# Gated cross-attention: keys split ahead of the diagonal, one product of the denominators a batch, taken in the next batch's step

## The reference

```python
qn = layernorm(x, ln_q_g, ln_q_b)
q = qn @ Wq * scale                       # 16 heads of 64
k, v = jnp.split(media @ Wkv, 2, axis=-1) # media: the context, 1500 keys
sim = jnp.einsum('bhid,bhjd->bhij', q, k)
sim = jnp.where(media_mask[:, None, None, :], sim, neg_inf)
attn = jax.nn.softmax(sim, axis=-1)
out = jnp.einsum('bhij,bhjd->bhid', attn, v)
x = x + jnp.tanh(attn_gate) * (out @ Wo)
h = jax.nn.gelu(layernorm(x, ln_ff_g, ln_ff_b) @ W1, approximate=False) @ W2
x = x + jnp.tanh(ff_gate) * h
```

## Time and profile before

| | |
|---|---|
| median of three executions | 1866.57 us |
| profiled execution | 1864.18 us, its span 1862.4 us |
| mean granted TensorE clock | 0.939 |
| busy: PE, DVE, ACT, POOL | 1596.7, 1010.7, 613.7, 515.2 us |
| 15 steps from batch 0 to the start of batch 15, first pass | 242.8 us, PE busy 225.3, DVE 126.4 |
| the same, second pass | 242.1 us |

### The profile page before, as it was taken

One profiled execution on the slowest core, in us unless ns is written; L12 is line 12 of the kernel. 1 busy time (PEld: TensorE's weight loads), 2 busy tenths in 40 slices (PEclk: granted clock), 3 DMA queues, 4 the chain that ended last, 5 costly groups with the idle time before them and its releaser, 6 DMA issues.

```text
span 1862.4 us, 29181 instructions
## 1 busy us (share of the span) xinstructions
PE 1596.7 (86%) x8106; PEld 829.9 (45%) x8107; DVE 1010.7 (54%) x1645; ACT 613.7 (33%) x992; POOL 515.2 (28%) x365
## 2 busy tenths in 40 slices
PE   7666588988988969989977898899986988999988
PEld 3233254554554534446633444444343444444434
DVE  6786467777777735213446555455323654555440
ACT  1131155555555530025532333333030322333211
POOL 1524056766766740000001022222001022222000
PEclk9877589999999979989988899999998989999999
DMA  6000512222222112013110000000031000000000
GB/s 220 0 1 1 125 50 70 65 79 64 67 78 62 30 42 77 0 59 108 66 60 19 1 28 26 25 25 2 1 93 55 1 18 18 25 25 18 2 1 20
DMA packets 46769, 80.37 MB, mean 43 GB/s; under 512 B 8616, under 2 KB 38584, under 8 KB 46648
## 3 DMA queue, kind: packets, MB, share of 16 engines
q1 hardware_dynamic: 46648, 78.96, 14.3%
HBM read 56.82 MB, written 0.92 MB: 31 GB/s over the span
## 4 chain that ended last, share of the span: by engine, by line
PE 72%; DVE 14%; issue 8%; ACT 2%; SPq 2%; POOL 1%; DVEq 1%; DMA 1%; ACTq 0%; POOLq 0%
PE psum L1705 21%; PE psum L2159 8%; PE psum L1859 5%; PE psum L2134 3%; PE psum L2165 3%; PE psum L1894 3%; DVE WA L1381 3%; PE psum L2259 3%; PE psum L2136 2%; PE psum L2020 2%; PE psum L1833 2%; PE psum L2151 2%; PE psum L1879 2%; SPq L530 2%; PE psum L2154 2%
## 5 line engine op out<-in xcount | busy, mean ns | idle before, releaser
L1381 DVE TENSOR_REDUCE WA<-psum 112x1 f32<-112x500 f32 x384 | 243.8, 676 | 75.9 <-PE psum L1859 73.4
L773 POOL TENSOR_TENSOR XN<-XN,WBZ 125x896 f32<-125x896 f32 x128 | 266.3, 2080 | 41.2 <-ACT WBZ L981 38.2
L981 ACT ACTIVATE WBZ<-psum 125x896 f32<-125x896 f32 x192 | 174.5, 917 | 173.3 <-PE psum L1879 166.4
L1119 ACT ACTIVATE WA<-psum,y_bias 125x448 f32<-125x448 f32 x192 | 120.7, 633 | 285.5 <-PE psum L2154 285.4
L2159 PE MATMUL psum<-WA,ctxN 125*128 125x448 f32 x384 | 181.0, 552 | 8.1 <-ACT WA L1119 8.1
L1859 PE MATMUL psum<-R 128*112 128x500 f16 x384 | 157.7, 414 | 32.7 <-DVE WA L1381 21.9
L804 POOL TENSOR_TENSOR XN<-const,y_max 112x896 bf16<-112x896 f32 x32 | 53.7, 1679 | 476.0 <-PE psum L2159 348.2
L1596 DVE TENSOR_REDUCE y_max<-psum 112x1 bf16<-112x375 f32 x256 | 130.9, 532 | 100.2 <-PE psum L2136 78.8
L2134 PE MATMUL psum<-XB,R 128*112 128x375 f16 x256 | 89.5, 350 | 32.9 <-DVE y_max L1596 24.5
L1879 PE MATMUL psum<-R 128*125 (+1 forms) x768 | 109.3, 266 | 0.7 <-ACT R L948 0.7
L1604 DVE RECIPROCAL WBZ<-WBZ (+1 forms) x68 | 104.4, 1540 | 2.3 <-DVE WBZ L1625 2.3
(11 more groups left out here) (256 smaller groups left out, 2744.3 us busy)
## 6 DMA issues: line engine op xcount, KB each, us to landing
R<-WA SPq DMA_DIRECT2D x192, 62.5 KB, 2.0
ctxT<-in_ctxT SPq DMA_DIRECT2D x12, 750.0 KB, 4.2
R<-in_ctxT SPq DMA_DIRECT2D x12, 750.0 KB, 5.5
WA<-in_ctxT SPq DMA_DIRECT2D x8, 750.0 KB, 4.1
R<-WA SPq DMA_DIRECT2D x192, 31.2 KB, 1.8
ctxT<-in_ctxT SPq DMA_DIRECT2D x32, 187.5 KB
ctxN<-in_ctx SPq DMA_DIRECT2D x32, 187.5 KB
WBZ<-in_x_w SPq DMA_DIRECT2D x4, 1024.0 KB, 6.5
```

Source lines behind the costliest of these rows:

```text
L773: nc.gpsimd.tensor_tensor(z_sum[p][0:TK, :], first[0:TK, :], z_p[t % 4][0:TK, :], ALU.add)\
L981: nc.scalar.activation(z_p[t % 4][0:TK, :].rearrange("p (k n) -> p k n", k=2), psum[0:TK, s:s + 2, 0:2 * GC], ACT.Exp, scale=float(CHD0) * ...
L1119: nc.scalar.activation(y_pT[t][0:TK, g * HALF:(g + 1) * HALF], bank[2 + u % 3][0:TK, 0:HALF], ACT.Exp, bias=y_bias[0:TK, bass.ds(b * NT + ...
L1381: V.tensor_reduce(z_mx[0:PR, r, c:c + 1], bank[4 + k % 2][0:PR, 0:PC], AX_X, ALU.max)\
```

## The change

POOL splits the keys of batch b + 2 ahead of the diagonal of b + 1, as soon as the first product of values of batch b - 1 is done. PE's second `sums` goes. DVE adds tile 2 to `y_sum` as well (`add_last`, at the end of its step, once the last exponential is there), and PE takes the one product left, `denominators(b)`, in the next step, between values 0 and behind 2. It reads the `y_sum` of batch b - 1. DVE's copy of bank 7 moves with it, from the end of the step to the place between maximum 1 and invert 0. ACT's first exponential of a step waits for the two adds of the batch before instead of its product. The first step of a pass now has such a product and copy too, and one more stands behind the last step. The code for further chunks is changed to match.

```diff
@@ gpsimd, step
+                    if nxt2:
+                        wait_alone(pool, "x2_pv", PARTS * (l * B + b) + 1)
+                        keys(b + 2, (s + 2) % SLOTS)
                     wait_alone(pool, "x2_pv", PARTS * (l * B + b) + PARTS)
                     if nxt:
                         diagonal(b + 1, 1 - p)
-                    if nxt2:
-                        keys(b + 2, (s + 2) % SLOTS)
...
@@ scalar, step
                             wait_alone(act, "x2_pv", PARTS * (l * B + b) + PARTS)
-                            wait_alone(act, "x2_dn", l * B + b + 1)
+                            wait_alone(act, "x2_dsum", 2 * (l * B + b) + 2)
...
@@ vector
-                def invert(b, g):
-
-                    if g == 0:
-                        wait_alone(dve, "x2_den", l * B + b + 1)
-                    part = y_den[:, bass.ds(b, 1), g * HALF // 2:(g + 1) * HALF // 2].rearrange("p b n -> p (b n)")
+                def denominators(k):
+
+                    wait_alone(dve, "x2_dn", l * (B + 1) + k + 1)
+                    V.tensor_copy(y_den[:, bass.ds(k, 1), :].rearrange("p b n -> p (b n)"), bank[7][:, 0:HALF])\
+                        .then_inc(sem("x2_den"), 1)
+                    wait_alone(dve, "x2_den", l * (B + 1) + k + 2)
+
+                def invert(k, g):
+                    part = y_den[:, bass.ds(k, 1), g * HALF // 2:(g + 1) * HALF // 2].rearrange("p b n -> p (b n)")
                     V.reciprocal(part, part).then_inc(sem("x2_inverted"), 1)
...
+                def add_last(b):
+                    wait_alone(dve, "x2_expd", PARTS * (l * B + b) + PARTS + 3)
+                    wait_alone(dve, "x2_dsum", 2 * (l * B + b) + 3)
+                    V.tensor_tensor(y_sum[0:TK, :], y_sum[0:TK, :], y_pT[2][0:TK, :], ALU.add)\
                         .then_inc(sem("x2_dsum"), 1)
...
                         if j == 1:
+                            denominators(b)
                             invert(b, 0)
...
-                    wait_alone(dve, "x2_dn", l * B + b + 2)
-                    den = y_den[:, bass.ds(b + 1, 1), :].rearrange("p b n -> p (b n)")
-                    V.tensor_copy(den, bank[7][:, 0:HALF]).then_inc(sem("x2_den"), 1)
+                    add_last(b)
...
                 over_batches(dve, batch)
+                denominators(B)
...
@@ tensor
-                def sums(src, rows, start, stop, dst):
-
+                def denominators(k):
+
+                    wait_alone(pe, "x2_dsum", 2 * (l * B + k) + 2)
+                    wait_alone(pe, "x2_den", l * (B + 1) + k + 1)
                     for j in range(2):
-                        mm = pe.matmul(dst[HDX * j:HDX * (j + 1), 0:HALF], ones[0:rows, 0:HDX],
-                                       src[0:rows, :].rearrange("p (r j s) -> p j r s", r=PAIRS, j=2)[:, j],
-                                       start=start, stop=stop)
-                    return mm
+                        mm = pe.matmul(bank[7][HDX * j:HDX * (j + 1), 0:HALF], ones[0:TK, 0:HDX],
+                                       y_sum[0:TK, :].rearrange("p (r j s) -> p j r s", r=PAIRS, j=2)[:, j],
+                                       start=True, stop=True)
+                    mm.then_inc(sem("x2_dn"), 1)
...
                     values(0)
+                    denominators(b)
                     behind(2)
...
                     values(4)
-                    wait_alone(pe, "x2_dsum", l * B + b + 1)
-                    wait_alone(pe, "x2_den", l * B + b + 1)
-                    sums(y_sum, TK, True, False, bank[7])
                     values(5)
-                    sums(y_pT[2], TK, False, True, bank[7]).then_inc(sem("x2_dn"), 1)
...
                 over_batches(pe, step)
+                denominators(B)
```

More of the change, by code:

```diff
@@ L492, in build @@
         PARTS = 2 * KT
-        EXTRA = 47
+        EXTRA = 49
         def over_batches(eng, step):
@@ L1167, in _ @@
             dve.sem_inc(sem("x2_den"), 1)
+            dve.sem_inc(sem("x2_dsum"), 2)
             V = nc.vector
@@ L1550, in _ @@
             more = entry(dve, T_MORE, MORE)
-            V.memset(y_den[:, 0, :], 1.0).then_inc(sem("x2_first_den"), 1)
-            dve.wait_ge(sem("x2_first_den"), 1)
+            V.memset(y_sum, 1.0).then_inc(sem("x2_first_sum"), 1)
             BX = 8
@@ L1641, in extra @@
                         for g in range(2):
-                            V.tensor_copy(y_wide[:, g * HALF:(g + 1) * HALF], bank[2 + g][:, 0:HALF])
-                        V.tensor_tensor(den, den, bank[4][:, 0:HALF], ALU.mult).then_inc(sem("x2_extra"), 1)
+                            half_g = slice(g * HALF, (g + 1) * HALF)
+                            V.tensor_copy(y_wide[:, half_g], bank[2 + g][:, 0:HALF])
+                            last = V.tensor_tensor(y_sum[0:TK, half_g], y_sum[0:TK, half_g], bank[2 + g][0:TK, 0:HALF],
+                                                   ALU.mult)
+                        last.then_inc(sem("x2_extra"), 1)
                         extra_step(dve, x, 27)
@@ L1652, in extra @@
                                             y_sofar[:, g * HALF:(g + 1) * HALF], ALU.add)
-                        V.tensor_tensor(den, den, bank[7][:, 0:HALF], ALU.add).then_inc(sem("x2_extra"), 1)
-                        extra_step(dve, x, EXTRA)
+                        for t in range(KT):
+                            V.tensor_tensor(y_sum[0:TK, :], y_sum[0:TK, :], y_pT[t][0:TK, :], ALU.add)\
+                                .then_inc(sem("x2_extra"), 1)
+                            extra_step(dve, x, 47 + t)
                     over_extras(dve, l, b, more, extra)
@@ L1688, in _ @@
             pe.sem_inc(sem("x2_pv"), PARTS)
-            pe.sem_inc(sem("x2_dn"), 1)
             pe.sem_inc(sem("x2_extra"), 1)
@@ L2113, in _ @@
             pe.wait_ge(sem("ones_ready"), 1)
+            pe.wait_ge(sem("x2_first_sum"), 1)
             with pe.Fori(0, 2) as l:
@@ L2222, in extra @@
                         for g in range(2):
-                            pe.matmul(bank[2 + g][:, 0:HALF], ones[0:PR, :], y_wide[0:PR, g * HALF:(g + 1) * HALF],
-                                      start=True, stop=True)
-                        sums(y_wide, PR, True, True, bank[4]).then_inc(sem("x2_extra"), 1)
+                            mm = pe.matmul(bank[2 + g][:, 0:HALF], ones[0:PR, :], y_wide[0:PR, g * HALF:(g + 1) * HALF],
+                                           start=True, stop=True)
+                        mm.then_inc(sem("x2_extra"), 1)
                         for u in range(PARTS):
@@ L2229, in extra @@
                             extra_step(pe, x, 30 + 3 * u)
-                            mm = attended(s, u)
-                            if u % 2 == 1:
-                                mm = sums(y_pT[u // 2], TK, u // 2 == 0, u // 2 == KT - 1, bank[7])
-                            mm.then_inc(sem("x2_extra"), 1)
+                            attended(s, u).then_inc(sem("x2_extra"), 1)
+                        extra_step(pe, x, EXTRA)
                     over_extras(pe, l, b, more, extra)
@@ L2241, in _ @@
                 over_batches(pe, step)
+                denominators(B)
                 wait_alone(pe, "x2_out", 2 * B * (l + 1) + 2)
-                wait_alone(pe, "x2_den", B * (l + 1) + 1)
+                wait_alone(pe, "x2_den", (B + 1) * (l + 1) + 1)
                 for m in range(XT + 1):
```

2 lines of the change are left out of this document (1 added, 1 removed).

## The result

| | median us | runs | ratio to before, 95% interval |
|---|---|---|---|
| before, run beside it | 1866.99 (1864.65 to 1871.23) | 4 | |
| after | 1915.44 (1910.21 to 1917.73) | 4 | 1.0259 [1.0239, 1.0278] |

The profiled execution of after is the 1910.21 us one, with a span of 1908.4 against 1862.4, so the spans have 46.0 us to explain. The mean granted clock is 0.940 against 0.939.

What follows compares the result with a forecast made beforehand. The step's end was taken as bound by PE's sequencer after the last exponential, not PE's array. 23.5 us a pass, 47 for both, plus 3 for the clock, on 1864.2 gave 1914 profiled, 1916 median; range 1880 to 1934.

Steps and rivals of the forecast that it cites:

- The step's end is the sequencer's: Ordinary step's end: turned 0 comes 2.68 us behind the last exponential, set by PE's sequencer; array then idle about 1.5.
- the two sums: Step's end: taking these products away frees 1.8 us of PE's array but is worth nothing.
- if the step's end shrinks: Stated sign of being wrong: the chain from behind 7 to the next turned 0 falling below 5.47 us.
- DVE's copy delays the maxima: Ordinary step: DVE waits 1.1 us for PE's product; maximum 2 is 2.04 late, the step 1.90 us longer.
- Keys ahead: Step's head: with POOL a step early, behind 0 gains 0.35 us and values 0 only 0.12.
- The other steps: Steps outside the ordinary ones: step 14 +1.1, step 0 +2.1, step 4 -1.2, step 8 +0.1, step 15 and behind +0.5 us.
- The clock: PE's clock might fall with the new idle times; a charge of 3 us was taken, nearer to step 8's case.
- A: Rival: PE's array is the bound, so the gain is real, 1.26 us a step: 1828 us; 7% for below 1863.
- B: Rival: DVE's delay is smaller, only the product is on the path: 1889 us; 17% including losses and gains cancelling.
- C: Rival: the clock falls again at the step's head, 1.5 us in a third to half of steps: about 1932; 15%.
- D: Rival: the jump over further chunks' code lands on code not yet there, 4.45 us six times: about 1935; 3%.

Runs made afterwards that it cites:

- experiment 2: After, with PE's second table load moved inside the step, between behind 3 and values 1, from behind the last exponential: 1894.26 us, ratio 1.0147.
- experiment 1: After, with DVE copying bank 7 only after maximum 3 and inverting both halves after maximum 7: 1878.09 us, ratio 1.0058.
- experiment 7: Before, with POOL's keys moved ahead of the diagonal and nothing else: 1859.65 us, ratio 0.9957.
- experiment 3: Before, without the product of y_sum with ones, so part of the computation is left out: 1861.08 us, ratio 0.996.
- experiment 10: experiment 5, with POOL's keys behind the diagonal again, as in before: 1926.99 us, ratio 1.032.
- experiment 5: After, with the edits of experiment 1 and experiment 2, next step's first table word behind turned 0, and PE's memset wait just ahead of its loop: 1846.71 us, ratio 0.9888.

## Why the prediction was right

**The step's end is the sequencer's.** Held for after: 1.50 us idle in the step followed where 1.5 was forecast, and experiment 2 shows that the sequencer's load sets the end there. For before it was nearly right. In the step that the prediction follows the two limits tie: the sequencer's record for turned 0 ends at 1102.98 and turned 0 starts at 1103.08. (The wait record in the earlier trace rows is that of 1098.6 to 1100.6; up to 1103.4 there are three.) In steps 5, 6, 9 and 10 the array is last by 0.17 us. So the two sums were not worth nothing: the chain from behind 7 to turned 0, which was to stay at 5.47, is 5.25 to 5.43 in seven of the nine ordinary steps ahead of step 12, and 5.1 instead of 5.45 in steps 12 and 13. By the prediction's own sign, "if the step's end shrinks", this small part was wrong.

**DVE's copy delays the maxima.** Held in every link: copy at 4.90 (forecast 4.97), idle 1.31 before it (1.1), maximum 2 at 7.15 (7.29), behind 4 with a wait of 1.01. Experiment 1 shows it as a cause: 37 of the 48 us go with the copy's and the inversions' place. With the other runs the ordinary step adds up: 1.20 for DVE's wait (experiment 1) and 0.90 for the product in PE's path (experiments 1 and 7), less 0.30 for the keys (7) and 0.17 at the end, is 1.63; measured are 1.6 to 1.8.

**Keys ahead.** Right in kind, mis-sized: "Values 0 gains less ... I take 0.12". In after it gained 0.14 to 0.30 in the nine ordinary steps ahead of 12. That accounts for a part of the shortfall: behind 7 came 1.83 us later in the mean of these steps, not 1.90, and the step's end took off another 0.11, so an ordinary step became 1.6 to 1.8 us longer. Over steps 0 to 14 of pass 1, 23.0 were forecast and 20.1 measured: 1.7 of the difference lie in the nine ordinary steps ahead of 12, and 1.1 in steps 12 and 13, which I had taken for ordinary and which grew by 1.2 and 1.5.

**The other steps.** Step 0 +2.2 (forecast 2.1), step 14 +0.9 and +0.8 (1.1), step 4 -1.3 and -1.4 (-1.2), step 8 +0.3 and +1.1 (0.1). For step 4 the clock was regained as forecast. But neither DVE's earlier return nor the moved copy is needed for it: experiment 7 has the same 18.63 us at 1.00 with the keys moved alone, and its DVE is idle for 5.40 us there, as in before (5.36).

**The clock.** I charged 3 us for it. Ordinary steps kept 1.00, as forecast. But it fell in step 8 of both passes, to 0.91, where step 8 of before had kept 1.00; the loss moved from step 4 to step 8, and so the mean over the 15 steps is 0.99 in both windows above. Steps 4 and 8 of after have the same program, and step 8 is 0.5 and 0.7 us the longer: about 1.1 us in all by my estimate, and most of step 8's excess.

**What was missing.** Outside steps 0 to 14 of the passes the spans differ by 5.1 us (3.2, 1.2 and 0.7) where I had 1.0. The memset's wait is 2.5 of that; the other 1.6 I can't name. (The start of pass 1 by itself says little: it lies between 1053.2 and 1062.8 us in the twelve traces, and PE's 500th matmul already between 145.1 and 151.6. Before and after agree at that matmul, 146.4 and 146.3.) Against it stand 5 us too many in the steps (46.0 forecast, 40.9 measured), and 3 for a clock whose loss in step 8 is in the 40.9. The sum forecast was 50, and the spans differ by 46.0; that the medians differ by 48.4 puts 1916 nearer to 1915.44 than the working deserves.

**The rivals.** A is refuted by the sign and by experiment 3; its premise, that PE's array ends the step, is true of before, but only by 0.2 us or less. B's mechanism exists, but it is what remains (0.90 us of product in PE's path, 0.45 a step net, experiment 1) when DVE's wait is gone. C: step 0 apart, where both kernels lose it (0.91 or so), the clock fell once in each pass, in step 8, and not in a third of the steps. D: no new stall at the forward jump; PE's "issue" waits ahead of turned 0 are 2.0 us at most in the 15 steps, in after as in experiment 1.

## What to carry to other kernels

A busy engine whose rows follow without a gap is the bound only if its sequencer would be done earlier: look for the records of loads, jumps and waits between the last data wait and the next instruction, and take from both limits together. On an engine that works in order, a short instruction that waits for another engine costs everything queued behind it; put it where its input is already there, and count the delay to the consumer of what stands behind. A piece of work may be worth little in one kernel and much in the next version of it, so an edit is worth retesting when its neighbours have changed. A step that keeps its length doesn't show that what was taken out was off the path: look whether another engine holds the next thing, as POOL did in experiment 3.

## What the runs showed of the hardware

**POOL is held up by DVE.** POOL's L795 took 1.17 us in before and 2.09 in after, with the same shape. Before, then after, pass 1 (ns min/median/max):

```profile
L795 POOL TENSOR_SCALAR ctxT<-ctxT x14: 1163/1167/1169, 1069.5 to 1279.9; 128x375 f32<-128x375 f32 x14
```

```profile
L795 POOL TENSOR_SCALAR ctxT<-ctxT x14: 1165/2094/2101, 1057.2 to 1286.2; 128x375 f32<-128x375 f32 x14
```

In after it starts together with DVE's second add, which has two inputs in SBUF and takes 1.09 us; DVE starts at 1109.64 and POOL at 1109.67:

```profile
1109.64 1.09 DVE L1619 TENSOR_TENSOR WA<-WA 125x896 f32<-125x896 f32 x1 [1.92 <-ACT WA L1120]
```

```profile
1109.67 2.10 POOL L795 TENSOR_SCALAR ctxT<-ctxT 128x375 f32<-128x375 f32 x1
```

The one record of the 14 that has no such add beside it, the first, is 1.17 us. POOL's others are longer by 0.92 us, somewhat less than the 1.06 that the add still runs, and the add's own is not longer. The Trainium skill, "SBUF — State Buffer", section "SBUF: two separate sides", says that a DVE instruction with two SBUF inputs and a GpSimd one that reads SBUF hold a shared pair of ports exclusively, so that the later one waits for the whole of the other. The trace agrees but for some 0.14 us. In after it cost nothing, since the keys are a step ahead. In experiment 10 it was in the path.

**PE's control work is dear.** One table word costs PE about 0.65 to 0.75 us at the point where it stands: by the records of after 0.65 from the start of its load (0.30 by itself) to the next instruction, 0.65 per step in experiment 2, and 0.76 by which behind 0 comes later in experiment 5. The compare and branch at the end of a step takes PE 0.21 us (at most 0.36 in after, 0.42 in before), DVE 0.056, ACT and POOL 0.045.

**The clock** kept 1.00 in ordinary steps of after, with 1.50 and 1.01 us idle in one step. Ahead of step 4 PE was idle for 2.02 us and the clock stayed at 1.00; ahead of step 8 it was idle for 1.86, and from 1201.50 to 1203.50 us the clock was 0.50, the lower level. In experiment 10 it fell to that level behind an idle of 2.71 us (0.52 from 1223.2 to 1226.0), and two steps with 2.56 and 2.72 us idle at the same place kept 1.00. These rows don't show what decides it; the length of one idle alone does not.
